# A ternary layer in another order, the top-64 loop with scores ahead of the old probabilities, and the second pair's statistics, norms and queries a step sooner

## The reference

```python
# L1_ffn: a layer norm ahead of it, tanh(g) times it added to x behind it
def bitlinear(x, W, b):
    w_scale = jnp.clip(jnp.mean(jnp.abs(W)), EPS, None)
    Wq = clip(round(W / w_scale), -1, 1) * w_scale
    x_scale = jnp.clip(jnp.max(jnp.abs(x), axis=-1, keepdims=True), EPS, None)
    xq = clip(round(x * (QB / x_scale)), -QB - 1, QB) * (x_scale / QB)
    return jnp.einsum('bnd,hd->bnh', xq, Wq) + b
h = bitlinear(x, W1, b1)              # 256 -> 1024
h = jax.nn.gelu(h, approximate=False)
return bitlinear(h, W2, b2)           # 1024 -> 256

# L2_xattn: 16 heads of 16, layer norm ahead, tanh(g) times it added behind
scores = jnp.einsum('bhqd,bhkd->bhqk', qh, kh) / np.sqrt(DHEAD)
# masked; the 64 largest of the 77 scores of a row are kept, then softmax
ctx = jnp.einsum('bhqk,bhkd->bhqd', probs, vh)
return ctx @ wo_w.T + wo_b
```

## Time and profile before

| | |
|---|---|
| median of three timed runs | 901.47 us |
| the three | 901.56, 901.47, 896.49 us |
| the profiled execution's own time | 897.16 us |
| its span | 895.4 us |
| busy: PE, DVE, ACT, POOL | 801.0, 655.2, 497.2, 531.4 us |
| mean granted clock of TensorE | 0.968 |
| ternary steps 13 to 17 on the trace's time | 230.4 to 269.3 us |
| top-64 items 0 to 31 on VectorE | 273.7 to 488.4 us |

### The profile page before, as it was taken

How to read it: one execution, slowest core, us unless ns; L and a number is a source line. 1 busy time by engine, 2 the same in 40 slices (tenths; PEclk the granted TensorE clock), 3 DMA queues, 4 the chain that set the end, 5 groups by cost and what they waited for, 6 DMA issues and landing times.

```text
span 895.4 us, 18961 instructions
## 1 busy us (share of the span) xinstructions
PE 801.0 (89%) x5858; PEld 628.7 (70%) x5858; DVE 655.2 (73%) x2739; ACT 497.2 (56%) x1287; POOL 531.4 (59%) x721
## 2 busy tenths in 40 slices
PE   6999998998788676867887989999999999998897
PEld 5677775886566444645666779788778879987775
DVE  4888686888979999999999873455455542516887
ACT  5778764568997797978877331222112122226673
POOL 3565644676752978878775125456455545237883
PEclk9999999999999697979999899999999999999999
DMA  9200001000000082000222621222222243140011
GB/s 296 62 1 2 2 1 48 1 1 1 1 1 1 2 328 97 1 25 2 71 72 87 227 72 36 37 42 43 37 42 43 36 87 58 19 107 1 13 36 48
DMA packets 37823, 46.70 MB, mean 52 GB/s; under 512 B 4327, under 2 KB 33871, under 8 KB 37724
## 3 DMA queue, kind: packets, MB, share of 16 engines
q1 hardware_dynamic: 29243, 35.77, 11.9%
q0 software_dynamic: 8480, 9.72, 7.1%
HBM read 33.80 MB, written 11.68 MB: 51 GB/s over the span
## 4 chain that ended last, share of the span: by engine, by line
PE 64%; DVE 14%; ACT 8%; issue 6%; POOL 6%; another core or an unknown queue 1%; DMA 1%; DVEq 0%; ACTq 0%; POOLq 0%; SPq 0%
PE ps L3012 10%; PE ps L3023 10%; PE ps L2358 4%; PE ps L2454 3%; PE ps L2481 3%; PE ps L2780 3%; PE ps L2800 3%; PE ps L3067 2%; PE ps L3041 2%; PE ps L2439 2%; ACT ptall L1254 2%; PE ps L2466 2%; DVE experts L1812 1%; PE ps L2811 1%; PE ps L2866 1%
## 5 line engine op out<-in xcount | busy, mean ns | idle before, releaser
L2080 DVE COPY ptall<-experts 128x512 f32 x136 | 53.3, 434 | 97.8 <-PE ps L3012 49.1
L1388 ACT ACTIVATE wk<-ps 128x1024 f32<-128x1024 f32 x34 | 34.9, 1025 | 131.3 <-PE ps L3012 69.1
L3012 PE MATMUL ps<-xnT,ptall 128*128 128x128 f32 x896 | 105.0, 275 | 2.3 <-DVE ptall L2080 1.8
L3012 PEld LDWEIGHTS ps<-xnT,ptall 128*128 128x128 f32 x896 | 102.4, 192 | 3.0 <-issue 3.0
L3023 PE MATMUL ps<-experts,wk 128*128 x448 | 102.0, 381 | 1.4 <-ACT xkeep L1398 1.4
L3023 PEld LDWEIGHTS ps<-experts,wk 128*128 128x128 f32 x448 | 82.9, 190 | 17.0 <-issue 6.8
L848 POOL DMA_INDIRECT xn<-expert_in,rown x34 | 36.0, 1058 | 80.7 <-PE ps L2998 57.1
L646 POOL TENSOR_TENSOR experts<-experts,rden 128x616 f32<-128x616 f32 x32 | 38.9, 1217 | 46.8 <-DVE rden L1572 46.8
L872 POOL DMA_INDIRECT token_sum<-xkeep,dest x28 | 47.6, 1699 | 31.1 <-ACT xkeep L1398 22.5
L1229 ACT ACTIVATE experts<-experts 128x77 f32<-128x77 f32 x248 | 62.1, 258 | 0.0
L2358 PE MATMUL ps<-ones 128*128 128x256 bf16 x434 | 55.7, 286 | 5.8 <-POOL mone L599 5.8
(11 more groups left out here) (382 smaller groups left out, 2358.5 us busy)
## 6 DMA issues: line engine op xcount, KB each, us to landing
experts<-in_ew SPq DMA_DIRECT2D x16, 1024.0 KB, 8.5
xkeep<-in_bw SPq DMA_DIRECT2D x2, 1024.0 KB, 7.3
expert_in<-xkeep SPq DMA_DIRECT2D x8, 256.0 KB, 3.9
x<-token_sum SPq DMA_DIRECT2D x8, 256.0 KB, 3.8
out<-x SPq DMA_DIRECT2D x7, 256.0 KB, 2.2
x<-in_x SPq DMA_DIRECT2D x1, 1536.0 KB, 9.1
...
```

Of the source, the lines that this page charges most:

```text
L2080: ins = nc.vector.tensor_copy(tilew[:, v, c, :], experts[:, bass.ds(e * EW + (c * FF + v * 512), 512)])
L3012: ins = nc.tensor.matmul(ps[j % 2][:, v, k * P:(k + 1) * P], tilew[:, v, c, k * P:(k + 1) * P], xTb[j % 3][:, c, :], start=c == 0, stop=c ...
```

## The change

- **Ternary layer.** On VectorE scaled 0 (k-10) goes ahead of largest 1 (k-11) and sum 1 (k-13). On TensorE first 0 (k-10) goes ahead of second 1 (k-13). Magic 1 leaves ScalarE's program; `mid_hidden` of tile 1 on GpSimd ends with the same computation as a tensor_scalar, with its waits.
- **Second pair.** `top_stats(1)` leaves VectorE's top-64 loop (behind item 1) and is done in two halves in k = 16 and 17 of the ternary phase. `top_scale(1)` on GpSimd and the two `top_norm` of pair 1 on ScalarE come one item sooner.
- **Top-64 loop.** Of item k-3 the eviction of the probabilities now stands in ScalarE's step k behind the scores' copy, and its values in TensorE's step k behind the scores (before, both were done for item k-2 at the end of step k). The copying out stands behind the exponentials. For k > LAST = 30 the old order holds, and in k = 30 both are done. The turn and the queries of the next pair stand on TensorE ahead of the turning of the probabilities, and their evictions on ScalarE in the same step, one step earlier than before.
- **Idle matmuls.** Late in the phase `top_probs` issues 14 matmuls without use ahead of its wait; in four items (those of `top_parts`, k = 26 to 29) it no longer does.
- **First expert logits.** The first of the later layer's turned tiles gets memory of its own (`xt_first`), and a wait on it goes; another wait moves into `top_values`.

```diff
--- before.py
+++ after.py
@@ -223,6 +223,7 @@
         hsel = sb("hsel", [P, 4 + 8 + 2])
         mrow8 = sb("mrow8", [P, NK], u8)
         mrow = arena(NK // 2).bitcast(bf16)
+        xt_first = arena(CH * S)
         mcol = sb("mcol", [P, B])
         msum, mneg, msq = (sb(n, [P, 2 * TB * CH]) for n in ("msum", "mneg", "msq"))
         wstat = sb("wstat", [P, 8])
@@ -443,10 +444,12 @@
         top_parts = {ITEMS * q + 10 + (m if q == PAIRS - 2 else (0, 4, 5, 6)[m]): 4 * q + m
                      for q in range(PAIRS - 1) for m in range(4)}
 
+        LAST = N4 - 2
+        TURN_EARLY = 0
         l5_at = {16: 0, 20: 1, 24: 2, 28: 3}
         l5_logit_at = {23: 0, 27: 1, 31: 2}
-        xT5 = [wk[0][:, CH * h:CH * h + CH, :].rearrange("p c s -> p (c s)").rearrange("p (t c s) -> p t c s", t=TB, c=CH)
-               for h in (1, 0, 0, 0)]
+        xt_rest = wk[0][:, 0:CH, :].rearrange("p c s -> p (c s)")
+        xT5 = [v.rearrange("p (t c s) -> p t c s", t=TB, c=CH) for v in (xt_first, xt_rest, xt_rest, xt_rest)]
 
         def l5_cols(b):
 
@@ -681,6 +684,13 @@
                 nc.gpsimd.tensor_scalar(big, big, EPS_Q, wstat[:, 5:6], ALU.max, ALU.mult)
                 gp.wait_ge(own_p.sem, n)
                 nc.gpsimd.tensor_tensor(fac, fac, mone[:, 0:1], ALU.pow).then_inc(ghs, 1)
+                if t:
+                    gp.wait_ge(ghs, TB * b + t + 1)
+                    gp.wait_ge(ghq, TB * b + t)
+                    if b:
+                        gp.wait_ge(ght, TB * b + t - 1)
+                    nc.gpsimd.tensor_scalar(hmag[t], hbuf[b % 2][t], fac, MAGIC, ALU.mult, ALU.add
+                                            ).then_inc(ghq, 1)
 
             gp.wait_ge(pv_p[0].sem, pv_p[0].past(SC))
             for h in range(2):
@@ -819,7 +829,7 @@
                     if k < N4 and j in (4, 5):
                         top_bias(q, j - 4)
                     if q + 1 < PAIRS:
-                        if q == 0 and j == 2:
+                        if q == 0 and j == 1:
                             top_scale(1)
                         if q and j == 0:
                             top_scale_late(q + 1)
@@ -1188,8 +1198,6 @@
                         ac.wait_ge(asp, B)
                     elif q == 1:
                         ac.wait_ge(done[3].sem, done[3].past(TT))
-                    elif q == 3 and p == 0:
-                        ac.wait_ge(lg_p.sem, lg_p.past(1))
                     for m in range(CH):
                         src = bank((4 if q else 2) + p)[:, m * S:(m + 1) * S]
                         nc.scalar.activation(top_wk(q, p, m), src, ACT.Identity,
@@ -1283,10 +1291,8 @@
                         mid_norm_f(k)
                     if 0 <= k - 6 < B:
                         mid_norm_g(k - 6)
-                    if 0 <= k - 11 < B:
-                        if k == B + 10:
-                            top_queries(0, 1)
-                        mid_magic(k - 11, 1)
+                    if k == B + 10:
+                        top_queries(0, 1)
                     if k == B + 11:
                         top_scores(1)
                         mid_hidden_t(B - 1, 1)
@@ -1316,13 +1322,16 @@
                 for k in range(N4 + 3):
                     if 1 <= k < N4 + 1:
                         top_abs(k - 1)
-                    q, j = (k - 1) // ITEMS + 1, (k - 1) % ITEMS
-                    if k >= 3 and (k - 3) // 2 % 2:
+                    ahead = k >= TURN_EARLY
+                    q, j = (k - 1 + ahead) // ITEMS + 1, (k - 1 + ahead) % ITEMS
+                    if k > LAST and (k - 3) // 2 % 2:
                         top_out(k - 3)
                     if k == N4 + 1:
                         l5_norm_tile(B // 2, 0)
                     if 1 <= k < N4 - 1:
                         top_scores(k + 1)
+                    if 3 <= k <= LAST:
+                        top_turned_probs(k - 3)
                     if 1 <= k < N4:
                         top_exp(k - 1, 0)
                     if k == N4:
@@ -1339,9 +1348,11 @@
                     if k == 1:
                         for c in range(CH):
                             keys2(1, c)
+                    if 3 <= k <= LAST and (k - 3) // 2 % 2:
+                        top_out(k - 3)
                     if k in top_parts:
                         top_residual(top_parts[k] // 4, top_parts[k] % 4, k)
-                    if 2 <= k < N4 + 2:
+                    if LAST <= k < N4 + 2:
                         top_turned_probs(k - 2)
                     if k - 1 in l5_at:
                         l5_norm(l5_at[k - 1])
@@ -1353,9 +1364,8 @@
                             top_total(pair, n + 7)
                         if -3 <= n < 1:
                             top_squares(pair, n + 3)
-                    early = 1 if k >= ITEMS else 2
-                    if k // ITEMS + 1 < PAIRS and 0 <= k % ITEMS - early < 2:
-                        top_norm(k // ITEMS + 1, k % ITEMS - early)
+                    if k // ITEMS + 1 < PAIRS and 0 <= k % ITEMS - 1 < 2:
+                        top_norm(k // ITEMS + 1, k % ITEMS - 1)
             if phases >= 5:
                 l5_turned(B // 2)
                 l5_norm(B // 2 + 1)
@@ -1945,26 +1955,26 @@
                         mid_quant(k - 8)
                     if 0 <= k - 2 < 4:
                         mid_values1(k - 2)
+                    if 0 <= k - 10 < B:
+                        mid_scaled(k - 10, 0)
                     if 0 <= k - 11 < B:
                         mid_largest(k - 11, 1)
                     if 0 <= k - 4 < B:
                         mid_values2(k - 4)
                     if 0 <= k - 13 < B - 2:
                         mid_sum_g(k - 13, 1)
-                    if 0 <= k - 10 < B:
-                        mid_scaled(k - 10, 0)
                     if 0 <= k - 4 < B:
                         mid_soft(k - 4)
                     if 0 <= k - 12 < B - 2:
                         mid_sum_g(k - 12, 0)
                     if k in (13, 14):
                         top_stats(0, [k - 13])
+                    if k in (B + 8, B + 9):
+                        top_stats(1, [k - B - 8])
                 drop_least(0)
                 for k in range(N4 + 2):
                     if 1 <= k < N4:
                         drop_least(k)
-                    if k == 1:
-                        top_stats(1)
                     if k == N4:
                         end_shift(N4 - 1)
                         end_norm(N4 - 2)
@@ -2785,15 +2795,15 @@
                     ins.then_inc(sc_p[4].sem, 1)
 
                 def top_probs(i):
-                    q, j = (i + 1) // ITEMS + 1, (i + 1) % ITEMS
+                    q, j = (i + 2) // ITEMS + 1, (i + 2) % ITEMS + (i + 2 >= TURN_EARLY)
                     pe.wait_ge(pt_s[4].sem, pt_s[4].past(i))
-                    if N4 - 9 <= i < N4 - 1:
+                    if N4 - 9 <= i < N4 - 1 and i + 2 not in top_parts:
                         warm(14, 4)
                     pe.wait_ge(nm_s, i + 1)
-                    if q < PAIRS and j == 3:
+                    if q < PAIRS and j == 4:
                         pe.wait_ge(xts[4].sem, xts[4].past(2 * q + 2))
-                    elif q < PAIRS and j in (4, 5):
-                        pe.wait_ge(q_s[4].sem, q_s[4].past(4 * q + 2 * (j - 3)))
+                    elif q < PAIRS and j in (5, 6):
+                        pe.wait_ge(q_s[4].sem, q_s[4].past(4 * q + 2 * (j - 4)))
                     for h in range(HG):
                         for t in range(TB):
                             at = (h % 2) * S + t * P
@@ -2804,6 +2814,8 @@
                 def top_values(i):
                     q, j, u = i // ITEMS, i % ITEMS, i % 2
                     s2 = j // 2 % 2
+                    if i - 1 in l5_at:
+                        pe.wait_ge(xts[5].sem, xts[5].past(l5_at[i - 1] + 1))
                     pe.wait_ge(pt_s[4].sem, pt_s[4].past(i + 1))
                     if s2 == 0 and i >= 4:
                         pe.wait_ge(oc_s, (i - 2) // 4 * 2 + u + 1)
@@ -2896,10 +2908,10 @@
                         mid_queries(k - 4, k)
                     if 0 <= k - 4 < B:
                         mid_values2(k - 4)
+                    if 0 <= k - 10 < B:
+                        mid_first(k - 10, 0)
                     if 0 <= k - 13 < B:
                         mid_second(k - 13, 1)
-                    if 0 <= k - 10 < B:
-                        mid_first(k - 10, 0)
                     if 0 <= k - 1 < 2:
                         mid_total(k - 1)
                     if k == B + 10:
@@ -2932,28 +2944,30 @@
                     if k == N4:
                         pe.wait_ge(sc_r[4].sem, sc_r[4].past(N4))
                         pe.wait_ge(done[4].sem, done[4].past(4 * (PAIRS - 1)))
+                    if 3 <= k <= LAST:
+                        top_values(k - 3)
                     if k in top_parts:
                         top_final(top_parts[k] // 4, top_parts[k] % 4, k)
```

(16 more changed lines are left out.)

## The result

| | before | after |
|---|---|---|
| median of 20 runs each | 899.37 us | 903.92 us |
| lowest, highest | 896.49, 904.28 | 900.03, 907.59 |
| ratio of the changed kernel to the kernel before | | 1.0038, 95% interval 1.0021 to 1.0054 |
| the profiled execution's own time, its span | 897.16, 895.4 | 900.88, 899.1 |
| mean granted clock of TensorE | 0.968 | 0.973 |

The change costs 0.4% (3.4 us by the ratio, 3.7 between the two profiled executions), where 0.9 less was forecast. The time is inside the range and within 1%; the sign is wrong. The table's last row says where the 3.9 us at item 31 come from: +3.2 by item 0, down to +1.6 by item 2, and back up to +3.9 over the 29 items behind it.

The account below looks back on a forecast made before the run. VectorE was taken to bound ternary steps 13 and 14 and nearly all the top-64 phase, waits steps 15 to 17; +3.8 - 1.1 - 1.6 - 3.8 + 1.8 = -0.9 from 899.2 gives 898.3 us, range 891 to 906.

Parts of the forecast that it names:

- Between the sums: Ternary steps 13 to 17: VectorE waits 1.30 for TensorE between sum 1 and sum 0, adding 3.8 us in all.
- Magic 1's relief: Ternary step 12: with magic 1 off ScalarE, 1.1 of VectorE's 1.5 us of waits goes.
- its price: Magic 1 on GpSimd takes 1.3 us, hidden before flip 1 of the next step wants it: cost 0.
- Statistics: The second pair's statistics leave VectorE behind item 1, saving 1.6 us; their halves hide in steps 16 and 17.
- The four old waits: Top-64 loop, items 2 to 31: VectorE's four waits all go with the later eviction of the probabilities, saving 3.8 us.
- The failing step: Top-64 loop at pair changes: ScalarE's item is 1.1 over twice, but 3.4 us of slack prevents a stall at full clock.
- +1.8 for one pair change: Top-64 loop, first pair change: half of a 3.5 us stall at the lower TensorE clock, bounds 0 and 10.5.
- Rival 2: Top-64 loop: same-item turn and queries at the lower clock starve VectorE at three pair changes, +10.5, about 907; chance 0.10.
- the ring of 7.63: Top-64 pair change, found after the run: ScalarE-TensorE chain from one absolute value to the next, 7.63 us at full clock.
- Rival 3: Top-64 loop: TensorE's own order brings the waits back, so the reordering gains nothing; +1.1, about 900; chance 0.15.
- Rival 1: Ternary steps 15 to 17: ScalarE was the bound, no wait between the sums appears; -9.9, about 889; chance 0.10.
- Rival 4: Ternary steps 13 to 15: quantiser meets GpSimd's magic, VectorE waits 1.3 in each; +3.0, about 902; chance 0.05.

Follow-up runs that it names:

- the magic alone: Kernel before with only magic 1 moved from ScalarE to GpSimd: 896.67 us, ratio 0.9973.
- the ternary change together: Kernel before with both ternary swaps and magic 1 on GpSimd, nothing else of the change: 901.85 us, ratio 1.0029.
- order and magic alone: Order: kernel before with only the two ternary swaps, magic 1 left on ScalarE, 904.01 us, ratio 1.0060. Magic: see the magic alone.
- the statistics alone: Kernel before with only the second pair's statistics, scale and norms early: 899.44 us, ratio 1.0002.
- the kernel with both repairs: Changed kernel with sum 1 ahead of scaled 0 and largest 1, second 1 ahead of first 0, turn and queries ahead of values and products: 889.75 us, ratio 0.9897.
- another kernel: Changed kernel with sum 1 ahead of scaled 0 and largest 1 on VectorE, second 1 ahead of first 0 on TensorE: 893.06 us, ratio 0.9941.

## Why the prediction was wrong, and where it was right

- **Between the sums** (+3.8 in steps 13 to 17): right. Measured +3.9; the wait is 1.22 where 1.30 was read. Per step 1.19, 1.19, 0.81, 0.36 and 0.37 against 1.30, 1.30, 0.82, 0.21 and 0.21.
- **Magic 1's relief** (-1.1) and its price (1.3 us, cost 0): the operation took 1.12. The Trainium skill (GPSIMD Engine Reference, Engine selection) has one-input work there at roughly line rate, which gave the estimate of 0.9; the measured 1.12 lies between that and the 1.3 read from the trace, and both hide. Steps 11 and 12 together gave 1.0. By the timed rounds the magic alone gave 2.4 (0.27%, interval 1.1 to 3.9), and the ternary change together cost 2.6 against the forecast 2.7. That this sum came out so close is in part luck: order and magic alone measured +5.4 and -2.4 where +3.8 and -1.1 were forecast. The prediction didn't see that magic 1, left on ScalarE, makes the swap 0.8 dearer in step 11.
- **Statistics** (-1.6): right at their place. Items 0 to 2 took 14.5 us in the changed kernel and with the statistics alone, 16.07 before. Alone they did not move the measured time.
- **The four old waits** (-3.8): those of items 12 and 31 went as said. Items 19 and 20 (1.0 and 0.74) still wait 0.28 and 0.98, and in the kernel with both repairs they don't.
- **The failing step: "The scores are copied some 3.0 after an item's start and wanted at 6.36: 3.4 of slack, no stall"** at the full clock, hence +1.8 for one pair change. The mechanism was named (values, queries and their eviction in one item), and its length was nearly right, 7.3 to 7.6 against "about 7.5". Two terms of it were mis-sized. The slack was counted inside one ideal item; but a copy of scores only comes early if ScalarE came early into the item, and it carried what the items ahead had left. Measured, the slack was 2.7 ahead of the first change and 1.5 ahead of the second. And the excess was counted as two items 1.1 over, 2.2 together; measured at the second change, four items from the turn on are over by 0.63 to 1.26 each, 3.8 together. In place of 1.8 stand waits of 6.3: 4.8 of them behind the three pair changes (items 7, 15, 16, 23), 1.5 at items 18 to 20. Items 2 to 31 were to take 2.0 less (-3.8 and +1.8) and took 2.25 more. With the measured 2.25 in place of these two terms the sum is +3.8 - 1.1 - 1.6 + 2.25 = +3.35, against +3.7 in the profiled execution and +3.4 by the ratio.
- Rival 2 had the place right (all three pair changes); its price of 10.5 is over twice the 4.8 measured there. Its reason, the lower clock, isn't needed, as the ring of 7.63 at 1.00 shows, but its mechanism is real: it adds to the first change, and with the queries at the lower level it made an item of 9.51 in another kernel. Rival 3 was near the truth of the loop: no gain of the new order alone is shown. Rival 1 fell: ScalarE's relief in steps 15 to 17 bought nothing. Rival 4 did not come about: the quantisers of steps 13 to 15 (from 232.91, 241.60 and 249.72) and GpSimd's magics (from 237.06, 245.75 and 253.87, 1.12 each) never ran at the same time. What two that meet would cost, no run here shows.
- I didn't ask whether the same edits could stand in another order. Each loss was undone by moving one piece: sum 1 ahead of two others, the turn and the queries ahead of the values.
